# A gated delta layer with a mixture of experts: blank rows written once at the end, and sums of squares by 128-column weights

## The reference

```
q = _l2norm(q) * DK ** (-0.5)          # _l2norm(x) = x * rsqrt(sum(x * x) + 1e-6), over 64 numbers of a head
k = _l2norm(k)
...
topk_w, topk_ids = lax.top_k(scores, K)                    # K = 4 of 32 experts
sort_idx = jnp.argsort(topk_ids.reshape(-1))
xs = jnp.take(flat, sort_idx // K, axis=0)                 # rows sorted by expert
gu = lax.ragged_dot(xs, w1, group_sizes)
ys = lax.ragged_dot(silu(g) * u, w2, group_sizes)
routed = sum over a token's four rows of ys * topk_w
```

## Time and profile before

| what | us |
|---|---|
| median of three runs | 1118.99 |
| the profiled execution, whole | 1115.1 |
| its span, first to last instruction | 1113.4 |
| PE busy | 969.2 (87%) |
| DVE busy | 672.8 (60%) |
| POOL busy | 620.2 (56%) |
| ACT busy | 491.2 (44%) |

### The profile page before, as it was taken

One profiled execution on the slowest core, in us unless ns is written; L12 is line 12 of the kernel. 1 busy time (PEld: TensorE's weight loads), 2 busy tenths in 40 slices (PEclk: granted clock), 3 DMA queues, 4 the chain that ended last, 5 costly groups with the idle time before them and its releaser, 6 DMA issues.

```text
span 1113.4 us, 31656 instructions
## 1 busy us (share of the span) xinstructions
PE 969.2 (87%) x12419; PEld 832.0 (75%) x12419; DVE 672.8 (60%) x1626; ACT 491.2 (44%) x938; POOL 620.2 (56%) x775
## 2 busy tenths in 40 slices
PE   3876899998999998899999989997487688999998
PEld 2764688788778788788877877887486355888887
DVE  6368947665766767586576658557824244444446
ACT  4533345453544545454354536343142222555552
POOL 3031238866885886787588568753314111665663
PEclk8687879779887988988797799869678798999999
DMA  6647027339565943946694380011052904444558
GB/s 244 205 101 210 1 50 196 116 101 252 156 177 153 275 135 89 282 119 182 171 255 135 78 229 16 25 50 35 30 209 75 362 29 133 134 148 149 154 183 294
DMA packets 181617, 165.32 MB, mean 148 GB/s; under 512 B 75219, under 2 KB 173916, under 8 KB 180576
## 3 DMA queue, kind: packets, MB, share of 16 engines
q10 hardware_dynamic: 70768, 72.65, 23.1%
q1 hardware_dynamic: 103072, 73.78, 22.4%
q0 software_dynamic: 7632, 16.87, 4.6%
HBM read 65.76 MB, written 101.55 MB: 150 GB/s over the span
## 4 chain that ended last, share of the span: by engine, by line
PE 49%; POOL 18%; DVE 12%; issue 8%; ACT 2%; DMA 2%; SPq 0%; POOLq 0%; DVEq 0%; ACTq 0%
PE ps L1653 7%; POOL arena L810 7%; POOL arena L807 6%; PE ps L1678 4%; PE ps L1563 4%; DVE arena L1146 4%; POOL nrm L773 3%; PE ps L1472 3%; PE ps L1428 3%; PE ps L1482 3%; PE ps L1492 3%; PE ps L1580 3%; PE ps L1644 2%; PE ps L1461 2%; PE ps L1541 2%
## 5 line engine op out<-in xcount | busy, mean ns | idle before, releaser
L1146 DVE SCALAR_TENSOR_TENSOR arena<-ps,cw,arena 128x256 f32<-128x256 f32 x384 | 155.3, 474 | 43.3 <-ACT arena L932 43.3
L1428 PE MATMUL ps<-work,arena 128*128 128x259 f32 x512 | 161.5, 472 | 15.4 <-DVE arena L1146 9.7
L1428 PEld LDWEIGHTS ps<-work,arena 128*128 128x128 f32 x512 | 117.1, 238 | 43.2 <-DVE arena L1146 11.2
L862 POOL DMA_INDIRECT picked<-work x95 | 94.3, 993 | 77.9 <-issue 57.1
L851 POOL DMA_INDIRECT slotted<-hr,slots x64 | 63.5, 993 | 101.7 <-DVE slots L1297 85.6
L810 POOL TENSOR_TENSOR arena<-arena 128x31 f32<-128x31 f32 (+15 forms) x186 | 109.9, 591 | 14.6
L1335 DVE TENSOR_TENSOR work<-work,ps 128x128 f32<-128x128 f32 (+1 forms) x111 | 34.1, 307 | 125.8 <-ACT work L1043 120.1
L807 POOL TENSOR_TENSOR arena<-arena 128x31 f32<-128x31 f32 (+15 forms) x186 | 95.0, 511 | 12.4
L1653 PE MATMUL ps<-arena,work 128*128 x380 | 97.8, 380 | 0.0
L932 ACT ACTIVATE arena<-ps,cw 128x256 f32<-128x256 f32 x128 | 58.0, 472 | 87.7 <-PE ps L1428 72.8
L832 POOL TENSOR_TENSOR work<-work,ec 128x512 f32<-128x512 f32 x32 | 34.0, 1062 | 88.8 <-PE ps L1521 66.2
(11 more groups left out here) (231 smaller groups left out, 2215.4 us busy)
## 6 DMA issues: line engine op xcount, KB each, us to landing
slotted<-blank ACTq DMA_DIRECT2D x17, 4128.0 KB, 18.9
arena<-in_w SPq DMA_DIRECT2D x2, 6528.0 KB, 27.3
arena<-tab SPq DMA_DIRECT2D x96, 128.0 KB, 4.5
work<-slotted SPq DMA_DIRECT2D x95, 129.0 KB, 2.1
arena<-picked SPq DMA_DIRECT2D x8, 1024.0 KB, 14.5
work<-tab SPq DMA_DIRECT2D x32, 128.0 KB, 3.7
arena<-in_w_qkv SPq DMA_DIRECT2D x1, 2048.0 KB, 7.5
xin<-in_x SPq DMA_DIRECT2D x16, 128.0 KB, 5.2
```

Source lines behind the costliest of these rows:

```text
L862: g.indirect_dma_start(out=picked, out_offset=bass.IndirectOffsetOnAxis(ap=to, axis=0), in_=yrow(j), in_offset=None, bounds_check=TOPK * T ...
L1146: v.scalar_tensor_tensor(out=acc_, in0=bank_of("proj", p, s_, i)[:, k:k + W2], scalar=cw[:, u, k:k + 1], in1=acc_, op0=ALU.mult, op1=ALU.a ...
L1428: ins = mm(to[:, 0:WX], wqkv[:, k, m:m + P], xt2[:, p % 3, k, :], start=k == 0, stop=k == KD - 1)
```

## The change: what it does

Three things.

1. The 17 transfers of blank rows by ACT, their semaphore wait in "send", and their places in the tables go. Instead, when the counts are known, DVE computes for every expert the first row behind its last one: `gap_first` (row of each expert) and `gap_at` (the same plus the partition's number), three instructions ahead of `spread_tiles`. POOL then scatters 128 blank rows for each of experts 0 to 11 by an indirect transfer, behind its last "send"; SP stores 128 blank rows for each of experts 12 to 31, reading the addresses into registers eight at a time. SP then waits for these 32 transfers before it loads a tile's row.
2. The products of "ss" take 128 tokens as weights and both columns of `parind`: 2 x 4 = 8 products for 32 in an item (16 for 64 in a pair).
3. The sums then lie in PSUM by token and head rather than by chunk and half, so "ssq" takes four DVE instructions of 64 partitions and 8 numbers for one of 128 and 16.

```
-                    pool.wait_ge(S["blank_sent"], 16 * (b + 2))
...
+                if name == "lists":
+                    pool.wait_ge(S["rows_out"], 1)
+                    for e in range(GAPS_ON_POOL):
+                        g.indirect_dma_start(out=slotted, out_offset=bass.IndirectOffsetOnAxis(ap=gap_at[:, e:e + 1], axis=0),
+                                             in_=blank, in_offset=None).then_inc(S["sent"], 16)
...
-                if (name, *ix) in BLANKS:
-                    t = BLANKS[name, *ix]
-                    act.wait_ge(S["blank_sent"], 16 * (t + 1))
-                    act.dma_start(by_rank[t * P:(t + 1) * P, :, :],
-                                  blank.unsqueeze(1).broadcast_to([P, E, WIDE])).then_inc(S["blank_sent"], 16)
...
+            sp.wait_ge(S["rows_out"], 1)
+            for e in range(GAPS_ON_POOL, E):
+                k = (e - GAPS_ON_POOL) % AHEAD
+                if k == 0:
+                    gaps = nc.values_load_multi_w_load_instructions(
+                        gap_first[0:1, e:min(e + AHEAD, E)], engines=(mybir.EngineType.SP,), min_val=0, max_val=E * STRIDE - P,
...
+                sp.dma_start(slotted[bass.ds(gaps[k], P), :], blank).then_inc(S["blank_sent"], 16)
             sp.wait_ge(S["table_out"], 1)
-            sp.wait_ge(S["sent"], 16 * TOPK * NB)
-            sp.wait_ge(S["blank_sent"], 16 * (NB + 2))
+            sp.wait_ge(S["sent"], 16 * (TOPK * NB + GAPS_ON_POOL))
+            sp.wait_ge(S["blank_sent"], 16 * (1 + E - GAPS_ON_POOL))
...
+                    to = to.rearrange("p (b e kt) -> p b e kt", b=2, e=2)
+                    per = bank_of("ss", p, kind)[:, 0:16].rearrange("p (b kt hp) -> p b kt hp", b=2, kt=KT)
+                    for hp in range(2):
+                        for e in range(2):
+                            ins = v.tensor_scalar(to[half(hp), :, e, :], per[half(e), :, :, hp], EPS, factor, ALU.add, ALU.mult)
+                    ins.then_inc(S["ssq_out"], 1)
...
+                v.tensor_tensor(gap_first, total, expert_at, ALU.add)
+                done(v.scalar_tensor_tensor(out=hot[:, 0, :], in0=total, scalar=me, in1=expert_at, op0=ALU.add, op1=ALU.add))
+                v.tensor_copy(gap_at, hot[:, 0, :]).then_inc(S["rows_out"], 1)
...
-                    for c in range(4):
+                    for b in range(2):
                         for kt in range(KT):
-                            for hp in range(2):
-                                ins = mm(to[half(hp), KT * c + kt:KT * c + kt + 1], sq[:, kt, C * c:C * c + C],
-                                         parind[:, hp:hp + 1], start=True, stop=True)
+                            at_ = 2 * (KT * b + kt)
+                            ins = mm(to[:, at_:at_ + 2], sq[:, kt, P * b:P * b + P], parind, start=True, stop=True)
```

More of the change, by code:

```diff
@@ L39 @@
 AHEAD = 8
+GAPS_ON_POOL = 12
 COUNTS_AT = 2 * SLOTS
@@ L59 @@
     "xload": [(-30.4,)],
-    "blank": [(-30.4,)],
     "mul": [(-29.2, 0, 0), (-28.8, 0, 1), (-23.7, 1, 0), (-23.3, 1, 1), (-18.9, 2, 0), (-18.5, 2, 1), (-9.3, 3, 0), (-8, 3, 1),
@@ L126 @@
     "send": [(199.1, 0), (235.3, 1)],
-    "blanks": [(199.2, 0), (235.3, 1)],
 }
@@ L201 @@
     "send": [(188.9, 0), (235, 1)],
-    "blanks": [(189, 0), (235.1, 1)],
 }
@@ L276 @@
     "send": [(177.5, 0), (200.5, 1)],
-    "blanks": [(177.5, 0), (200.5, 1)],
 }
@@ L281 @@
 PER_BLOCK = ("osq", "nin", "npow", "yn", "yt", "yg", "op", "x2", "xin", "lnp", "xn", "rmp", "hh", "base", "hr", "ht", "htb", "rt", "mx", "ex",
-             "tk", "rank", "slot", "send", "blanks")
+             "tk", "rank", "slot", "send")
 FILL = ("nin", "yn", "op", "x2", "xn", "hh", "rt", "mx", "tk", "rank", "slot")
@@ L345 @@
 SCHEDULE = schedule()
-BLANKS = {item: t for t, item in enumerate([item for item in SCHEDULE if item[0] in ("blank", "blanks")][:NB + 1])}
 AFTER_SUM = {"ht": "htb_in", "rt": "rt_in", "rank": "rank_in"}
@@ L555, in gated_delta_moe @@
         lane = sb("lane", 8)
+        gap_at = sb("gap_at", E, dt=U32)
+        gap_first = sb("gap_first", E, dt=I32)
         table = sb("table", 2, P, dt=I32)
@@ L565, in gated_delta_moe @@
         O, U = (KS, QS), (UR, W[3])
-        by_rank = slotted[0:E * STRIDE, :].rearrange("(e r) w -> r e w", e=E)
         s_in, s_wq, s_w, s_pool, s_vch = (sem(n) for n in ("inputs_loaded", "projection_loaded", "weights_loaded", "pool_steps", "vector_steps"))
@@ L691, in _ @@
                 stage(*item)
+            sp.wait_ge(S["rows_out"], 1)
[4 more added lines that the diff above has]
+                        gap_first[0:1, e:min(e + AHEAD, E)], engines=(mybir.EngineType.SP,), min_val=0, max_val=E * STRIDE - P,
+                        skip_runtime_bounds_check_because="an expert has at most T rows of its STRIDE")[1]
+                sp.dma_start(slotted[bass.ds(gaps[k], P), :], blank).then_inc(S["blank_sent"], 16)
             sp.wait_ge(S["table_out"], 1)
-            sp.wait_ge(S["sent"], 16 * TOPK * NB)
-            sp.wait_ge(S["blank_sent"], 16 * (NB + 2))
+            sp.wait_ge(S["sent"], 16 * (TOPK * NB + GAPS_ON_POOL))
+            sp.wait_ge(S["blank_sent"], 16 * (1 + E - GAPS_ON_POOL))
             sent_rows = []
@@ L1152, in stage @@
                         wait(dve, S["rn_out"], p)
-                        v.tensor_scalar(rin, bank_of("ss", p, kind)[:, 0:16], EPS, None, ALU.add).then_inc(S["ssq_out"], 1)
+                        to, factor = rin, 1.0
                     else:
                         wait(dve, S["nin_out"], 2 * (p - 3))
-                        v.tensor_scalar(rn[:, p % 4, 16:32], bank_of("ss", p, kind)[:, 0:16], EPS, EPS * DH, ALU.add,
-                                        ALU.mult).then_inc(S["ssq_out"], 1)
+                        to, factor = rn[:, p % 4, 16:32], EPS * DH
+                    to = to.rearrange("p (b e kt) -> p b e kt", b=2, e=2)
[4 more added lines that the diff above has]
+                    ins.then_inc(S["ssq_out"], 1)
                 if name == "kn":
@@ L1606, in tail @@
                 if name == "rows":
-                    pe.wait_ge(S["rows_out"], 1)
+                    pe.wait_ge(S["rows_out"], 2)
                     tr(W3[0:1, 2 * P:3 * P], lane[:, 3:4], ident)
```

## The result

| | kernel before | changed kernel |
|---|---|---|
| median, us | 1113.4 (20 runs, 1105.4 to 1121.3) | 1117.2 (20 runs, 1115.7 to 1119.2) |
| ratio to before | | 1.0041, interval 1.0022 to 1.0060 |
| profiled execution, us (span) | 1115.1 (1113.4) | 1117.8 (1116.0) |

The change makes the kernel slower, by 0.2 to 0.6%. The direction was forecast; the time, 1127.2 us with a range from 1119.5, was not. One part of the miss is the level: the three runs of before known at the time had a median of 1118.99, and 20 have 1113.4. Against that the change costs 3.8 us, where 8.2 were forecast. The 4.4 us between the two hide larger errors that partly cancel.

The account below looks back on a forecast made before the run. No engine bounds the whole: PE, POOL and DVE take turns, then PE alone from 940 us. Loop -6.0 and end +14.2 us gave +8.2 on a median of 1118.99: 1127.2 us, range 1119.5 to 1136.

Parts of the forecast that it names:

- Part 4, the end: Blank rows written after the counts delay tile 0 on PE: 14.2 us lost, bounds 10.5 and 38.
- Part 1, the sums: Sums of squares on PE take half as long per item; the loop gains 6.0 us, bounds 0 and 10.
- PE saves nothing: Rival: old items already overlap their two halves, so the loop's 6.0 us fall away, 1133.2 us; chance 0.15.
- the taps' idle time: DVE's waits for ACT ahead of taps cap what arrives from PE: 5.0 us over six pairs, plus 1.0 in the opening.
- the next limit that I named: Once PE is earlier than the taps need, DVE's queue limits: transposes wait for POOL, 2.14 us in one pair.
- my bound: Loop gain at most 10 us: 1.0 and seven kind-1 items at 1.3 us, without DVE or POOL in the way.
- Part 2, the evictions: Four DVE instructions for one after the sums: costed at nothing in six pairs; 8 us if not hidden.
- Part 3, the blank rows that go: Removing 17 blank-row transfers of 18.9 us each from the loop gains 0, bounds 0 to 2 us.
- The clock: Rival: shorter sums let PE's clock return sooner in its own stretch, up to 17 us gained, time 1110; chance 0.09.
- The sum: Loop gain and end cost added: -6.0 + 14.2 = +8.2 us, forecasting a median of 1127.2 us.

Follow-up runs that it names:

- the two orders of the same 16 products: Changed kernel, each sums-of-squares product split into two with 64-token weights: output halves alternating, 1106.9 us; all lower-half products before upper-half ones, 1115.2 us.
- The run with halves in turn: Changed kernel, each sums-of-squares product split into two with 64-token weights, written alternately to lower and upper partitions: 1106.9 us, ratio 0.9947.
- early blank rows: Kernel before, blank rows left in the loop, with 16 sums-of-squares products of 64-token weights alternating between partition halves, and four evictions: 1104.0 us, ratio 0.9943.
- late blank rows: Changed kernel with old sums of squares, blank rows only at the end, plus three spare DVE instructions ahead of each eviction: 1115.9 us, ratio 1.0032.
- the unread transfers: Changed kernel, with ACT again issuing the 17 transfers of 4128 KB at their old places, into a tensor nothing reads: 1127.4 us, ratio 1.0139.

## Why the prediction was wrong

- **Part 4, the end: right.** POOL's pace of 1.27 us, SP done first, a wait for a scatter, PE's stop of 13.35 us and the lower clock behind it: 14.6 us, forecast 14.2. That part carried the direction. Missing in it was that the pieces fill the transfer engines: the last scatter landed 3.7 us after its start, for 2.4 forecast.
- **Part 1, the sums: wrong.** The step that failed is "twice a record's price and a quarter of the records: 1.0 and 1.75 us, half of before". The 66 cycles a record (76 at the full clock, 32 ns), which I read as 64 columns that load alone, are the price of a record that overlaps with its neighbour: alone, with its neighbour in the same half, a record of 64 columns takes 1.82 us / 32 = 57 ns, and 3.18 / 32 = 99 ns at the lower clock. The rival "PE saves nothing" had this mechanism and I gave it 0.15. The Trainium skill, "TensorE: Matmul & The Clock Gate", Part 3, has the rule (products whose outputs lie in distinct column groups run at once), and here the two orders of the same 16 products show it, 1.10 and 1.82 us an item. What these rows could not tell me was which of two readings of 66 cycles holds; the other row with 128-column weights, 0.22 us for two records, gave 1.76 us an item, 0.08 from what came, and I set it aside for a reason (two columns for 32) that had no row.
- **What of a shorter item arrives: too little.** By the taps' idle time I gave half an item 6.0 us. The run with halves in turn gained 10.3. Its traces show the next limit that I named, DVE's transposes waiting for POOL, 2 to 3 us in most pairs (DVE in time, two of them), but a little later than my bound. The mean clock rose with it, to 0.872 from 0.864 (and to 0.877 from 0.868 with early blank rows), so how much of the 10.3 is the shorter item and how much the clock is not told apart. The waits:

```profile
412.40 1.25 DVE L1215 STREAM_TRANSPOSE arena<-arena 128x1024 f32<-128x1024 f32 x1 [3.00 <-POOL arena L812]
...
692.35 1.25 DVE L1215 STREAM_TRANSPOSE arena<-arena 128x1024 f32<-128x1024 f32 x1 [3.04 <-POOL arena L812]
```

  In the changed kernel these waits are short or absent, and the taps still wait for ACT (1.53 us, DVE in time):

```profile
325.15 2.44 DVE L1147 SCALAR_TENSOR_TENSOR arena<-ps,cw,arena 128x256 f32<-128x256 f32 x6 [1.53 <-ACT arena L933]
```

- **Part 2, the evictions: right**, at nothing, as far as late blank rows show it.
- **Part 3, the blank rows that go: wrong.** The step is "I take 0; bounds 0 to 2 us of gain"; it is about 10. I argued that no step of the chain waits for a transfer, and compared two stretches of 2 us. Both hold for what they show. But I never listed PE's stops without a releaser and what is in flight in each. The page doesn't show them: its 8% of "issue" in the chain are 8% in the changed kernel too. Only PE in time does. Why PE stops there, no run shows.
- **The clock:** the rival had the changed kernel gain by it; its mean over the runs is 0.864 for 0.868 to 0.870 in before. Nothing gained, as its sums did not get shorter; where they did, with the halves in turn, the clock rose.
- **The sum.** -1.5 (sums, by the run that undoes them) - 10.2 (traffic) + 14.6 (end) = +2.9 us; measured 3.8. That two errors of 4.5 and 10.2 in opposite directions left +8.2 only 4.4 off is luck. The level of 5.6 us is no mechanism, but it is a step of the sum that failed: I forecast from the median of three runs and left room for "the 3 us by which runs differ", and before's 20 runs differ by 16.

## What to carry to other kernels

Before a small product is widened, look at whether neighbours already alternate between halves of the output partitions: a record in such a row cost 32 to 34 ns here, for 57 alone, and widening it won next to nothing. Transfers that nobody waits for can still cost: look for entries that stop inside an item with no releaser, and see what is in flight there. And a wait at the end of this kernel is paid one for one, while a third of a millisecond of transfers spread through the loop cost 10 us: moving work out of a loop is worth only what it costs there.

## What the runs showed of the hardware that I had not expected

- 64-column float32 weights with two columns to multiply: 34 ns a record when neighbours alternate halves (1.10 us / 32), 57 ns when they don't, and 115 ns for 128 columns (1.84 / 16), at the full clock.
- While the blank transfers keep the 16 engines full (DMA share 0.97 to 1.10 in before's stops), PE stops between products, for up to 2.3 us in before and 2.7 with the unread transfers. What PE lacks then no view names. The page of before lists two queues of the kind "instruction" (q8, 1.67 MB, and q14, 0.35 MB); that PE's instructions come late through them would fit and was not tried.
- SP's stores of 128 rows slow down in a long row: less 0.73 us a reading, 0.45 us each for 12, 0.50 for 20, 0.64 for 25, and 0.84 for 14 when ACT issues as well; in the stretches shown above the transfer engines are at 0.97 to 1.11.
- The time of a run of before goes with its mean granted clock: in one group of 35 the shortest has 1102.1 us at 0.879, one of the longest 1119.8 at 0.861. The 20 runs of the changed kernel, with its quiet loop, stay within 3.5 us.
